# An LSTM layer with residual: 8 plain steps instead of 16, differences of the weights formed on GpSimd, and another order of the first transfers

## The reference

```python
def _L0_cond_ref(x, h0, Wx, Wh, b):
    Hdim = h0.shape[1]
    c0 = jnp.zeros_like(h0)
    xW = jnp.einsum('ntd,dk->tnk', x, Wx) + b
    def step(carry, xw_t):
        prev_h, prev_c = carry
        a = xw_t + prev_h @ Wh
        i = jax.nn.sigmoid(a[:, :Hdim])
        f = jax.nn.sigmoid(a[:, Hdim:2 * Hdim])
        o = jax.nn.sigmoid(a[:, 2 * Hdim:3 * Hdim])
        g = jnp.tanh(a[:, 3 * Hdim:])
        next_c = f * prev_c + i * g
        next_h = o * jnp.tanh(next_c)
        return ((next_h, next_c), next_h)
    _, hs = jax.lax.scan(step, (h0, c0), xW)
    return jnp.transpose(hs, (1, 0, 2))
x = x + _L0_cond_ref(x, cond_1024, L0_cond_Wx, L0_cond_Wh, L0_cond_b)
```

## Time and profile before

| | |
|---|---|
| median of 3 runs | 2569.0 us (2568.67 to 2570.64) |
| profiled execution | 2573.19 us, its span 2571.4 us |
| TensorE matmul busy | 2540.0 us, 99% |
| VectorE busy | 1949.6 us, 76% |
| ScalarE busy | 1026.7 us, 40% |
| GpSimd busy | 0.2 us |
| HBM read, written | 42.27 MB, 33.55 MB |

### The profile page before, as it was taken

How to read it: one execution, slowest core, us unless ns; L and a number is a source line. 1 busy time by engine, 2 the same in 40 slices (tenths; PEclk the granted TensorE clock), 3 DMA queues, 4 the chain that set the end, 5 groups by cost and what they waited for, 6 DMA issues and landing times.

```text
span 2571.4 us, 201742 instructions
## 1 busy us (share of the span) xinstructions
PE 2540.0 (99%) x92454; PEld 2497.3 (97%) x92454; DVE 1949.6 (76%) x6292; ACT 1026.7 (40%) x3249; POOL 0.2 (0%) x4
## 2 busy tenths in 40 slices
PE   7999999999999999999999999999999999999998
PEld 5899999999999999999999999999999999999998
DVE  7777777777777777777777777777777777777775
ACT  5433343333433443343344334333433343343332
POOL 0000000000000000000000000000000000000000
PEclk9999999999999999999999999999999999999999
DMA  4011010010110110100101101101001011011000
GB/s 171 22 34 33 16 33 25 24 33 18 31 33 16 33 33 16 33 24 24 33 17 32 33 16 33 33 16 33 24 24 33 17 32 33 16 33 33 16 16 18
DMA packets 141236, 76.60 MB, mean 30 GB/s; under 512 B 8452, under 2 KB 140164, under 8 KB 140164
## 3 DMA queue, kind: packets, MB, share of 16 engines
q1 hardware_dynamic: 141056, 75.79, 11.2%
q10 hardware_dynamic: 132, 0.07, 0.0%
HBM read 42.27 MB, written 33.55 MB: 29 GB/s over the span
## 4 chain that ended last, share of the span: by engine, by line
PE 98%; DMA 1%; issue 0%; DVE 0%; SPq 0%; ACT 0%; DVEq 0%
PE if_odd L237 25%; PE og_odd L244 13%; PE if_even L244 13%; PE if_odd L244 13%; PE og_even L244 13%; PE s1t_sum L237 6%; PE og_even L237 6%; PE if_even L237 6%; DMA w_raw<-in_L_cond_Wh_dram 1%; PE og_odd L253 0%; PE if_odd L253 0%; PE if_even L253 0%; PE og_even L253 0%; SPq L215 0%; DVE hw_lo L632 0%
## 5 line engine op out<-in xcount | busy, mean ns | idle before, releaser
L568 DVE TENSOR_TENSOR i_g<-i_f,g_gate 128x128 f32<-128x128 f32 x512 | 149.9, 293 | 427.0 <-ACT g_gate L424 427.0
L237 PE MATMUL if_odd<-xw_hi,xT_lo 128*32 128x256 f16 x7936 | 426.8, 273 | 0.1
L237 PE MATMUL if_odd<-xw_lo,xT_hi 128*32 128x256 f16 x7936 | 426.8, 273 | 0.1
L237 PE MATMUL if_odd<-xw_hi,xT_hi 128*32 128x256 f16 x7936 | 426.8, 273 | 0.1
L237 PEld LDWEIGHTS if_odd<-xw_lo,xT_hi 128*32 128x32 f16 x7936 | 252.4, 97 | 0.4 <-issue 0.3
L237 PEld LDWEIGHTS if_odd<-xw_hi,xT_lo 128*32 128x32 f16 x7936 | 252.2, 97 | 0.5 <-issue 0.4
L237 PEld LDWEIGHTS if_odd<-xw_hi,xT_hi 128*32 128x32 f16 x7936 | 252.3, 97 | 0.3 <-issue 0.3
L432 ACT ACTIVATE tanh_c<-c_state 128x128 f32<-128x128 f32 x512 | 159.1, 311 | 195.9 <-DVE c_state L570 195.9
L421 ACT ACTIVATE i_f<-if_odd 128x256 f32<-128x256 f32 x256 | 98.7, 386 | 237.2 <-PE if_odd L244 237.2
L393 ACT ACTIVATE if_even<-if_odd 128x256 f32<-128x256 f32 x248 | 91.3, 368 | 253.9 <-PE if_odd L237 253.9
L244 PE MATMUL if_even<-hw_lo,hT_hi 128*32 128x256 f16 x4096 | 168.0, 273 | 8.2 <-DVE hw_lo L632 4.9
(11 more groups left out here) (110 smaller groups left out, 6062.4 us busy)
## 6 DMA issues: line engine op xcount, KB each, us to landing
x_ring<-in_x_dram SPq DMA_DIRECT2D x256, 128.0 KB, 2.8
out_dram<-x_ring SPq DMA_DIRECT2D x252, 128.0 KB, 2.1
w_raw<-in_L_cond_Wx_dram SPq DMA_DIRECT2D x4, 1024.0 KB, 8.1
w_raw<-in_L_cond_Wh_dram SPq DMA_DIRECT2D x4, 1024.0 KB, 16.6
out_dram<-x_ring SPq DMA_DIRECT2D x8, 64.0 KB, 1.8
bias_raw<-in_L_cond_b_dram SPq DMA_DIRECT2D x4, 64.0 KB, 2.9
h_raw<-in_cond_dram ACTq DMA_DIRECT2D x1, 64.0 KB
```

What stands on the lines that cost most here:

```text
L237: mm = nc.tensor.matmul(bank[j * N:(j + 1) * N, 0:HALF], x_part[:, pair, n, k * N:(k + 1) * N], w_part[:, n, k, j, :], start=start and g = ...
L568: nc.vector.tensor_tensor(i_g[:, :], i_f[:, 0:P], g_gate[:, :], ALU.mult).then_inc(i_g_ready, 1)
```

## The change

`PLAIN` becomes 8. The eight halves of the four formed matrices are made by GpSimd, in the order S3, S1, S2, A22, each in the place of a quarter that is already split; S3 is formed as B22 - B12, so that it needs no other formed matrix, and S2 as B21 + S3. VectorE splits the low part of one half in each of steps 0 to 7; ScalarE splits the high part of the first half ahead of the last piece of `Wh` and of one half in each of steps 0 to 6. GpSimd also casts h0, makes the remainders `xp_lo` of the eight plain steps and `bias_diff`. The bias is loaded from ScalarE's queue, ahead of h0. SyncE issues x of steps 8 on after the last weight piece has landed. `hw_hi_ready` now counts quarters, so that VectorE's split of a quarter waits for that quarter alone (TensorE still waits for all four).

```diff
-PLAIN = 16
+PLAIN = 8
...
+           P_S3: (2, 1), P_S1: (0, 1), P_S2: (0, 0), P_A22: (2, 0)}
+FORMED = (P_S3, P_S1, P_S2, P_A22)
...
             for n in range(2 * J):
                 sp.dma_start(w_raw[:, n, :], w_v[n]).then_inc(w_loaded[n], 16)
+            sp.wait_ge(w_loaded[2 * J - 1], 16)
             for c in range(1, SLOTS):
...
-                    pe.wait_ge(hw_hi_ready, k + 1)
+                    pe.wait_ge(hw_hi_ready, (k + 1) * J)
...
-                if plain_steps > 0:
-                    n, k = (P_S1, P_S2, P_S3, P_A22)[t // 4], t % 4 - 1
-                    if 0 <= k < 2:
-                        act.wait_ge(w_diff_ready, t // 4 * 2 + k + 1)
-                        split_x_hi(n, *W_PLACE[n], k)
+                if plain_steps > 1:
+                    split_formed(t + 1)
+
+            def split_formed(piece):
+                act.wait_ge(w_diff_ready, piece + 1)
+                n, k = FORMED[piece // 2], piece % 2
+                split_x_hi(n, *W_PLACE[n], k)
...
             def split_h_lo(k):
-                dve.wait_ge(hw_hi_ready, k + 1)
...
                 for j in range(J):
+                    dve.wait_ge(hw_hi_ready, k * J + j + 1)
                     v = split_lo(src[:, j, :, :], hi[:, j, :, :], lo[:, j, :, :])
...
+        @block.gpsimd
+        def _(pool):
+            def rest_plain(t):
+                pool.wait_ge(xp_hi_ready, t + 1)
+                first = (A11, A21)[t % 2]
+                lo, hi = [a[:, t, :, :].rearrange("p (h k) e -> p h (k e)", h=2) for a in (xp_lo, xp_hi)]
+                nc.gpsimd.tensor_tensor(lo, x_blocks[:, t // GROUP % 2, t // 2 % 2, first:first + 5:4, :], hi,
+                                        ALU.subtract).then_inc(xp_ready, 1)
+            def raw(k, gates):
+                return w_raw[:, k, gates * HALF * J:(gates + 1) * HALF * J]
+            def form(n, k):
+                k0, gates = W_PLACE[n]
+                place = raw(k0 + k, gates)
+                a, b, op, was, formed = {P_S3: (place, raw(k, 1), ALU.subtract, W_B22, 0),
+                                         P_S1: (place, raw(k, 0), ALU.subtract, W_B12, k + 1),
+                                         P_S2: (raw(2 + k, 1), place, ALU.add, W_B11, 2 + k + 1),
+                                         P_A22: (place, raw(k, 0), ALU.subtract, W_B21, 4 + k + 1)}[n]
+                pool.wait_ge(xw_hi_ready[was], k + 1)
+                pool.wait_ge(xw_lo_ready[was], k + 1)
+                if formed:
+                    pool.wait_ge(w_diff_ready, formed)
+                nc.gpsimd.tensor_tensor(place, a, b, op).then_inc(w_diff_ready, 1)
...
+            for t in range(PLAIN):
+                rest_plain(t)
...
+            for n in FORMED:
+                for k in range(2):
+                    form(n, k)
```

More of the change, by code:

```diff
@@ L262, in plain @@
                         for k in range(J):
-                            plain_add(banks[half], part, half, w, t % GROUP, k)
+                            plain_add(banks[half], part, half, w, t, k)
             def keep_going():
@@ L470, in split_h_hi @@
                 for j in range(J):
-                    a = split_hi(src[:, j, :, :], dst[:, j, :, :])
-                a.then_inc(hw_hi_ready, 1)
+                    split_hi(src[:, j, :, :], dst[:, j, :, :]).then_inc(hw_hi_ready, 1)
+            for j in range(J):
+                src = bias.rearrange("(o g f) -> o g f", o=1, g=GATES)[:, :, j * P:(j + 1) * P]
+                act.dma_start(bias_raw[j * N:(j + 1) * N, :].rearrange("p (g f) -> p g f", g=GATES),
+                             src.broadcast_to([N, GATES, P])).then_inc(bias_loaded, 16)
             act.dma_start(h0_raw[:, :], h0.rearrange("n (j f) -> j n f", j=J)).then_inc(h0_loaded, 16)
@@ L477, in _ @@
             copy_x(0)
[L478 to L481, removed]
+            act.wait_ge(w_loaded[0], 16)
+            split_x_hi(W_B11, *W_PLACE[W_B11], 0)
+            cast_plain(0)
+            split_x_hi(W_B12, *W_PLACE[W_B12], 0)
             act.wait_ge(bias_loaded, 16 * J)
@@ L484, in _ @@
             seed_plain(0)
-            seed_plain(1)
-            for k in range(J):
+            act.wait_ge(x_blocks_ready, 2)
+            copy_x(1)
+            for k in range(1, J):
                 act.wait_ge(w_loaded[k], 16)
@@ L489, in _ @@
                     split_x_hi(n, *W_PLACE[n], k % 2)
+                if k == 1:
+                    for t in range(1, PLAIN):
+                        cast_plain(t)
+                if k == 2:
+                    seed_plain(1)
             for k in range(J):
@@ L492, in _ @@
                 split_h_hi(k)
+                if k == J - 2:
+                    split_formed(0)
             for t in range(PLAIN):
@@ L524, in combine_rest @@
                 combine(group, g, S4, A12, S2, ALU.subtract, 5)
-            def rest_plain(t):
-                dve.wait_ge(xp_hi_ready, t + 1)
-                first = (A11, A21)[t % 2]
-                lo, hi = [a[:, t % GROUP, :, :].rearrange("p (h k) e -> p h (k e)", h=2) for a in (xp_lo, xp_hi)]
-                nc.vector.tensor_tensor(lo, x_blocks[:, t // GROUP % 2, t // 2 % 2, first:first + 5:4, :], hi,
-                                        ALU.subtract).then_inc(xp_ready, 1)
             def rest_early(q, pair):
@@ L680, in _ @@
                     split_x_lo(n, *W_PLACE[n], k % 2)
+                if k == 0:
+                    transpose_x(1, 1, 0)
+                    transpose_x(1, 1, 1)
+                if k == 2:
+                    transpose_h(h_hi_ready, h_hi, hT_hi, hT_hi_ready, 1)
+                    transpose_h(h_lo_ready, h_lo, hT_lo, hT_lo_ready, 1)
             for k in range(J):
```

63 lines of the change are left out of this document (15 added, 48 removed).

## The result

The kernel after takes 2584.6 us (median of 4 runs, 2582.4 to 2586.4) against 2569.1 us before (4 runs, 2568.7 to 2570.6): a ratio of 1.0052, with a 95% interval of 1.0040 to 1.0064. It is slower, by 10 to 16 us, 0.4 to 0.6%. The prediction was 2560.5, its range ended at 2582.5, so both sign and range were missed. What happened is rival (b), GpSimd and VectorE shutting each other out. It was priced at +2 to +15; the medians differ by 15.5, just above that, and the two profiled executions by 10.0.

A forecast was written before the change was run, and what follows sets the result against it. TensorE, 98% of the chain that ended last, was taken to bound the kernel. -6.4 (steps) - 2.1 (start) = -8.5 took the profiled 2573.2 us to 2564.7; the median, 4.2 lower, gave 2560.5, range 2557.5 to 2582.5.

The forecast's parts named there:

- rival (b): At the start, GpSimd's forms and VectorE's splits exclude each other: +2 to +15 us, middle +8.5, 2577.5; chance 0.33.
- the sum's silent term: Work moved to GpSimd was taken to cost VectorE nothing, so the sum held no term for it.
- the deadlines: When ScalarE wants GpSimd's forms: up to 7.6 us allowed for the first, about 5.5 for each further one.
- (a): Likeliest case: all terms hold and GpSimd is in time; 2560.5 us, range 2557.5 to 2564.5; chance 0.46.
- Eight steps leave the plain form: -6.4: Eight steps move from unrolled code (5.71 us) to the loop's pace (4.91): 2.6 us from matmuls, 3.8 from gaps.
- In steps 0 to 7, nothing: ScalarE's added formed high parts and VectorE's half-splits in these steps cost nothing; TensorE's slack is 0.43 us.
- The start: -2.1: Before step 0's last product, VectorE's weight splits end at 33.0 us instead of 35.13, with waits by quarters.
- The bias on ScalarE's queue: Bias leaves SyncE's queue, first weight issued at 2.7 us, not 4.60: credited nothing, bound 1.9 us.
- Sharing at half pace (c): VectorE runs at half pace while GpSimd reads; start 6.5 us later, -2 in all, 2567; chance 0.14.
- GpSimd late (d): Forms over 7.6 us make ScalarE, VectorE and TensorE wait: +6 at 8 us a form, +13 at 9; chance 0.07.

The follow-up runs named there:

- a6: The kernel after with only the bias put back on SyncE's queue; 2582.8 us, ratio 1.0045.
- b5: The kernel before with VectorE waiting for single quarters of hw_hi and x of steps 8 on issued behind the weights; 2570.0 us, ratio 0.9989.
- a1: The kernel after with the eight forms (halves of formed matrices) alone moved from GpSimd to VectorE; 2566.8 us, ratio 0.9980.
- a2: The kernel after with all GpSimd work on VectorE, forms spread over steps, and h0 ahead of the bias on ScalarE's queue; 2568.0 us, ratio 0.9986.
- a5: a2 with the bias back on SyncE's queue, ahead of the weights; 2565.4 us, ratio 0.9974.
- a7: a5 with x of steps 8 on no longer issued behind the weights; 2566.0 us, ratio 0.9977.
- b1: The kernel before with waits by quarters, x of steps 8 on behind the weights, and the bias on ScalarE's queue behind h0; 2573.4 us, ratio 1.0004.
- a4: The kernel after with each GpSimd form cut into four instructions of 256 columns; 2577.7 us, ratio 1.0023.
- a3: The kernel after with each GpSimd form computed twice, the first time into a place nobody reads; 2602.2 us, ratio 1.0117.

## Why the prediction was wrong

**The step that failed** is the sum's silent term: what GpSimd does was taken to cost VectorE nothing. With it goes the chance of only 0.33 for the case in which it costs something, "GpSimd and VectorE shut each other out". The forms were placed rightly, in the stretch where VectorE ends last and has no idle time, and their exclusion was priced. But the likeliest case was built on the deadlines, which only say when GpSimd's results are wanted. They don't say what it does to its neighbour while it makes them. "Against it the rows have nothing" was said of (b), and they had nothing for (a) either: no GpSimd work stood beside VectorE in them, and (a) was still given 0.46 against 0.33. What the runs show in its place: a form holds each waiting split up for 2.13 us, eight of them for 17.0, and with the smaller work hw_lo ends 18.0 us later. The Trainium skill (SBUF — State Buffer, section Who interferes with whom) has the rule, for a VectorE instruction with two inputs in SBUF against a GpSimd instruction that reads there and not against one that only writes. The traces here agree: 2.13 us of turn for a form, nothing for 24 memsets, nothing for a transpose.

**Its size in (b).** I put 17 in the middle of 10 to 24. It was 17.0 for the forms and 2.3 for the smaller work, 19.4. A form's turn is 2.13 us; 2.2 was assumed, and an estimate from the Trainium skill (GPSIMD Engine Reference, section 3.1 Elementwise) was 2.25. The sum by that page came to 2579.5, nearer than my 2577.5. The eight turns were all paid in full, since each of the eight forms stood against a waiting split.

**Eight steps leave the plain form: -6.4.** Right in its direction and its parts, and a little small: 8.1 was measured. Between step 1 and step 40 the six kernels with 16 plain steps need 205.1 to 209.2 us, 208.0 in the mean; after and a6 199.9 and 198.9. That is 8.6 less, where execution differs from execution by 2. The matmuls are 2.6 of it as computed. The gaps fell by more than the 3.8 allowed: the waits of the weight loads for "issue" add up to 10.9 us before (from 36 to 246 us) and 4.3 after (54 to 256). In b5, whose steps were short, they are 7.3.

**In steps 0 to 7, nothing.** Right with the forms away from VectorE: from step 1 to step 8 before needs 38.9 us and after 39.1. With a form in each step on VectorE (a1, a2, a5, a7) it is 41.8 to 43.5. The slack of 0.43 us that the prediction read the earlier trace rows doesn't hide 1.2.

**The start: -2.1.** Too much by 0.7 in this kernel. VectorE's last idle moment ends at 18.21 and not near 17.5, and 15.5 us of work from there end at 33.7, 1.4 under before. The first weight piece was issued at 2.63 instead of 4.60, yet ScalarE had it at 10.6 and not at 9.8. That a5 ends hw_lo at 32.8, close to the 33.0 of the forecast, is partly luck: its third piece of splits starts at 18.3, and it has no transposes of h0 (0.6) behind that. a7 shows that the weights' landing hardly counts there, and b5 that 3.7 was to be had with 16 plain steps.

**The bias on ScalarE's queue: "I give that nothing."** Wrong, and the other way from its bound. It was weighed as a gain for SyncE's queue. What moved is that 0.25 MB in small packets now stand in ScalarE's queue beside the weights in SyncE's. What comes first in ScalarE's queue is still in time: in the kernel after the bias lands 3.6 to 6.1 us after its issue. What comes second is late: there h0, at 19.0 instead of 4.7; in a2 and b1, where h0 is first, the bias. The price is 1.8 us at hw_lo's end (a2 against a5) and 5.3 (b1 against b5). In the kernel after it is covered for the most part by the forms' stall (a6: 1.2 us).

**Sharing at half pace (c)** is out by a4 (same bytes, 12 us less) and by a3 (the forms show less time beside shorter instructions). **GpSimd late (d)** happened, by another way than a slow form. The forms were to start at about 20.0; they start at 29.1, since h0 lands late and the remainders stand ahead of them. ScalarE waits 3.38 us for the first form and the last hw_hi is made at 34.6, but VectorE was far behind by then and went on for another 18 us.

The whole with measured terms, all from the trace of after: -1.4 for the start without turns, +17.0 and +2.3 from turns, -8.1 from the steps: +9.8, against +10.0 in the spans. The other 5 us between the medians are not accounted for by name. They are of the size by which executions of one kernel differ (the kernel before: 2568.0 to 2576.3 over the runs beside these experiments).

## What to carry over

Before work goes to GpSimd "for free", look what VectorE does at that time. In this kernel it was bound there and had two inputs from SBUF in nearly every instruction, and each GpSimd instruction that read SBUF cost it nearly its whole length: 2.13 us for a form, even where the VectorE instruction was one of 0.28. The eight forms are 9.8 us of work on VectorE itself (8 x 1.22), spread over steps with some slack, and cost 17 us when "offloaded". Where it must be, cut the GpSimd instructions small (a4 got back 7.5 us), or put them where VectorE has one-input work; the second wasn't run by itself.

A small early transfer is safe ahead of the big ones on their own queue (the bias: 3.0 us). On another queue beside them only what was first came in time; the last bias transfer took 10.7 us there and h0 16.3.

## What was not expected of the hardware

- The turns are strict. Over eight forms the order was one form, one split, each time. GpSimd never got two turns in a row while VectorE had a two-input instruction waiting, nor the other way. The durations in the trace (2.79 and 2.83 us) hold the wait, so both engines look busy at 100% and slow.
- A small part of each GpSimd instruction doesn't hold VectorE up. Two that ran without a two-input instruction beside them, a remainder of the kernel after and a piece of a4:

```profile
21.28 0.43 POOL L663 TENSOR_TENSOR xp_lo<-x_blocks,xp_hi 128x128 f16<-128x128 f32 x1
```

```profile
41.41 0.73 POOL L683 TENSOR_TENSOR w_raw<-w_raw 128x256 f32<-128x256 f32 x1
```

  Against splits, their turns are 0.22 us (splits 0.835 apart instead of 0.61) and 0.53 (1.13 apart instead of 0.60). The difference is 0.2 in both, which is why cutting a form in four doesn't add to what it holds up (4 x 0.53 against 2.13) but does to GpSimd's own time.
- What stands second in ScalarE's queue comes very late beside the weights. The page's queue table of the kernel after (packets, MB, share) shows it small:

```profile
q10 hardware_dynamic: 708, 0.33, 0.1%
```

  It was 132 packets before, with h0 alone. These 0.33 MB finish at 19.0 us, 16.3 after h0's issue, while SyncE's queue brings 8 MB of weights from 2.6 to 28.4. The Trainium skill (DMA: Bandwidth & Descriptors, section Queues, rings and completion order) says that a transfer engine goes round its queues packet by packet. If so, a queue of small packets moves few bytes a turn, which would give such a delay; this is an inference, and no run here tests it. The traces agree in direction; how many bytes of the weights pass for each small packet isn't settled by them.
- TensorE's clock at half through most of the stall (0.63 from 31 to 53 us) cost nothing visible afterwards: 3.3 us from hw_lo's end to step 1's product, 3.2 before. It was back at 1.00 from 54 us on.
- The unrolled code's "issue" gaps differ between executions of near-identical kernels (205.1 to 209.2 us for steps 1 to 40 with 16 plain steps), while from step 16 to step 32, in the loop, all eight kernels with 8 plain steps need 78.60 or 78.61. This is likely the scatter of the medians; it was not tested by itself.
